# Prologue of a transformer block: packed constants, a short first norm, and batch 3's projections spread over the first scores

## The chip, the cores and the metric

The kernel runs as one program on one core of a Trainium2 chip. The core has TensorE (PE: matmuls; PEld: its weight loads), VectorE (DVE), ScalarE (ACT), GpSimd (POOL) and SyncE (SP), which here issues all DMAs. Each engine works through its own list of instructions in order and waits on semaphores. The metric is the time of one execution on the device, in microseconds (us), lower is better.

## What is computed

Attention with 16 heads of 8 over 16 batches of 256 tokens, width 128, then a mixture of experts, each with a norm ahead, a norm behind and a residual. Cut to what matters here:

```python
x = x + layernorm(attention(layernorm(x)))     # x: 16 x 256 x 128
x = x + layernorm(ffn(layernorm(x)))           # router, 32 experts, top 6, and a shared expert
# attention: q, k, v = xn @ w.T + b ; softmax(q k / sqrt(8)) v ; @ w_o.T + b_o
```

## The kernel before

**Tiles and batches.** `NB` = 16 batches of `T` = 256 tokens; a batch is `TH` = 2 tiles of 128 tokens. x stays in `xbig`. A batch has `NU` / `NB` = 2 units of scores, each of `UB` = 4 steps k with two heads packed into the array's halves, so that there are 32 units, u = 0 to 31.

**What a batch needs before its scores.** Normalise its two tiles (`norm_x`: `xn`), transpose them on PE (`transpose_x`, L1159, through `pX`), keep the result (`keep_xnT`, ACT), project q and k (L1164, L1167, both halves of the one bank `pX`). The float32 results are then cut into three bf16 parts: `part1` (ACT, L627 and L630), `rest` (DVE, L845, reads `pX` and writes `q_rest` and `k_rest`, of which there is one buffer each), `part2` (ACT for the first batches, POOL later), `part3` (L317, L318: on DVE for batches 0 and 1, on POOL from batch 2 on). SP writes the parts to DRAM (`write_parts`, L381, six DMAs) and reads them back in another layout as one unit of scores at a time (`load_unit`, L393, four DMAs, into a ring of `RING` = 6 slots).

**Scores are made twice.** `query_scores` (L1179, into three banks `pS1`) give the row maxima, which DVE takes (`row_max`, L865, two for each k). When a unit's eight maxima are there, POOL cuts them into parts (`split_max`, L499 to L502), PE transposes these (`transpose_max`, L1243, through `pX`), ACT copies them out (`keep_mT`), and SP puts them into the unit's slot (`load_max`, L401). Only then can `key_scores` (L1185) give the scores less their maxima, whose exponentials ACT takes (L655).

**The order, written out by hand.** PE projects batches 0 to 2, then computes query scores of units 0 to 2 (`LEAD` = 3). Among these lie `transpose_max(0)` behind k = 1 of unit 1, `project(3)` (all of batch 3's transposes and projections) behind k = 2 of unit 1, and `transpose_max(1)` behind k = 1 of unit 2. In the main loop, step j = 0 to 7 of batch b pairs key scores of unit 2b + j // 4 with query scores of unit 2b + 3 + j // 4; from j = 4 on there are also the outputs (L1235). So the loop's first step needs unit 3 in its slot, and j = 4 of batch 0 needs unit 4.

**SP's queue.** After the loads of x and of the constants: `write_parts(0)`, `load_unit(0)`, `load_unit(1)`, `write_parts(1)`, `load_unit(2)`, `load_max(0)`, `load_unit(3)`, `write_parts(2)`, `load_max(1)`, `load_unit(4)`, `load_unit(5)`, `write_parts(3)`, and so on (L404 to L436). `write_parts(b)` waits for `part3`, `load_unit(2b)` for the landing of b's parts, `load_max(u)` for `keep_mT(u)`.

**POOL's queue.** Memsets (the slots of the ring, `m_zero`, `power`, the pads, and the two large ones of `vv`, L489), the chain of the norm for batches 1 to 3 (`chain_x(0)`), `split_max(0)`, `part3(2)`, the chain for the batches from 4 on (`chain_x(1)`), `split_max(1)`, ...

**The first norm.** DVE takes the statistics of batch 0's tiles (L1041), then a chain of 20 small instructions (`norm_chain` with `fused=True`, L327 to L347), with an inverse root by three Newton steps; ACT normalises (L603).

## Time and profile before

| | |
|---|---|
| median of 3 runs | 531.38 us (530.69 to 531.44) |
| the profiled execution, its own time | 531.55 us |
| its span, first to last instruction | 529.5 us |
| mean granted TensorE clock | 0.994 |
| PE, busy share of the span | 91% |
| DVE, ACT, POOL | 76%, 67%, 32% |
| busy tenths of PE in the first four fortieths of the span | 2, 4, 5, 6 |
| the same, fifth fortieth to the end | nearly all 9 |

A fortieth is 13.2 us. The rows of the timeline give the start of an instruction, how long it took, the engine, the line, what it writes and reads; "x4" merges four in a row, and the square brackets tell how long the engine had been idle and what ended that. SPq is the queue on which SP issues DMAs: its rows are the issuing alone, the data move later.

### The profile page before, as it was taken

The page shows a single profiled execution, that of the slowest core. Times are in us where ns is not written, and L with a number is a line of the kernel's source. Part 1 is how long each engine was busy: PE and PEld are TensorE (multiplying, and loading weights), DVE is VectorE, ACT ScalarE, POOL GpSimd, SP SyncE. Part 2 cuts the span into 40 slices and gives each one's busy share as a digit, 9 for nine tenths or more (in the row PEclk, how much of TensorE's full clock was granted, in tenths as well). Part 3 has the DMA queues.
Part 4 walks back from the last instruction along what each step waited for, and adds up shares of the span by engine and source line. Part 5 has one row for each costly group of instructions (what it writes and reads, how often), then busy time and mean ns, then how long its engine had stood idle before and what let it go on. Part 6 is the DMA issues. An engine that isn't in the chain of part 4 may idle for free.

```text
span 529.5 us, 10851 instructions
## 1 busy us (share of the span) xinstructions
PE 479.3 (91%) x3376; PEld 268.1 (51%) x3376; DVE 400.7 (76%) x1074; ACT 354.9 (67%) x701; POOL 171.8 (32%) x501
## 2 busy tenths in 40 slices
PE   2456999999998999998799999999999999999994
PEld 1222445454444445444346666666656665666662
DVE  4678788899999989888926769596776859585453
ACT  2423788888889988887675566767667666755442
POOL 5045133333535535211002324425153533302021
PEclk9999999999999999999899999999999999999999
DMA  6334444444444344330042244535363544535431
GB/s 177 114 122 127 120 130 132 125 134 131 131 143 137 117 120 122 121 107 32 4 142 68 114 164 157 167 104 200 94 186 108 179 160 138 197 106 176 142 107 40
DMA packets 52744, 67.47 MB, mean 127 GB/s; under 512 B 4560, under 2 KB 36304, under 8 KB 52688
## 3 DMA queue, kind: packets, MB, share of 16 engines
q1 hardware_dynamic: 52688, 66.78, 40.5%
q8 instruction: 28, 0.46, 0.4%
q14 instruction: 28, 0.23, 0.2%
HBM read 51.17 MB, written 15.20 MB: 125 GB/s over the span
## 4 chain that ended last, share of the span: by engine, by line
PE 73%; DVE 9%; ACT 6%; issue 6%; POOL 5%; DMA 0%; POOLq 0%; DVEq 0%; ACTq 0%
PE pS L1316 12%; PE pY L1316 11%; PE pO L1235 8%; PE pS L1179 7%; PE pS L1300 6%; PE pS L1302 6%; PE pS L1301 6%; DVE mneg L865 4%; PE pS L1185 3%; ACT probs L655 3%; PE pX L1164 2%; PE pX L1167 2%; PE pX L1159 1%; PE pY L1262 1%; POOL xn L524 1%
## 5 line engine op out<-in xcount | busy, mean ns | idle before, releaser
L865 DVE TENSOR_REDUCE mneg<-pS 128x2 f32<-128x512 f32 x256 | 164.0, 685 | 23.4 <-PE pS L1179 22.7
L655 ACT ACTIVATE probs<-pS 128x512 f32<-128x512 f32 x256 | 144.2, 595 | 25.6 <-PE pS L1185 23.9
L730 ACT ACTIVATE h_ring<-r 128x512 f32<-128x512 f32 x144 | 90.4, 629 | 88.9 <-DVE r L1034 68.0
L1034 DVE SCALAR_TENSOR_TENSOR r<-pS,c_ring 128x512 f32<-128x512 f32 x128 | 87.6, 689 | 45.6 <-PE pS L1302 44.2
L1179 PE MATMUL pS<-kp,qp 48*128 48x256 bf16 x512 | 87.5, 291 | 18.8 <-DVE mneg L865 10.1
L1300 PE MATMUL pS<-qp,up_hi 128*128 128x512 f32 x144 | 103.5, 719 | 0.0
L1185 PE MATMUL pS<-qp,kp 51*128 51x256 bf16 x512 | 87.6, 282 | 0.9 <-ACT probs L655 0.7
L1235 PE MATMUL pO<-probs,vv 128*32 128x256 f32 x1024 | 74.1, 397 | 0.4 <-ACT oT_sb L606 0.4
L1316 PE MATMUL pS<-h_ring,down_sb 128*128 128x512 f32 x144 | 73.8, 594 | 0.0
L1316 PE MATMUL pY<-h_ring,down_sb 128*128 128x512 f32 x144 | 73.4, 595 | 0.0
L1179 PEld LDWEIGHTS pS<-kp,qp 48*128 48x128 bf16 x512 | 34.1, 96 | 69.0 <-DVE mneg L865 40.5
L1302 PE MATMUL pS<-qp,up_lo 128*128 128x512 f32 x144 | 57.0, 396 | 0.0
L1301 PE MATMUL pS<-kp,up_hi 128*128 128x512 f32 x144 | 56.7, 394 | 0.0
L1300 PEld LDWEIGHTS pS<-qp,up_hi 128*128 128x128 f32 x144 | 27.3, 189 | 27.3 <-issue 25.8
L1301 PEld LDWEIGHTS pS<-kp,up_hi 128*128 128x128 f32 x144 | 27.4, 190 | 26.4 <-issue 26.4
L499 POOL TENSOR_TENSOR m_parts<-mneg,m_zero 128x16 bf16<-128x16 f32 x32 | 7.0, 220 | 102.2 <-DVE mneg L865 102.2
L1235 PEld LDWEIGHTS pO<-probs,vv 128*32 128x32 f32 x1024 | 25.6, 110 | 27.1 <-issue 18.8
L1185 PEld LDWEIGHTS pS<-qp,kp 51*128 51x128 bf16 x512 | 33.0, 96 | 7.5 <-ACT probs L655 4.9
L545 POOL TENSOR_TENSOR xbig<-xbig,yn 128x512 f32<-128x512 f32 x8 | 10.5, 1311 | 67.0 <-ACT yn L603 67.0
L1316 PEld LDWEIGHTS pY<-h_ring,down_sb 128*128 128x128 f32 x144 | 27.0, 189 | 8.3 <-issue 1.4
L1316 PEld LDWEIGHTS pS<-h_ring,down_sb 128*128 128x128 f32 x144 | 27.1, 189 | 6.8 <-ACT h_ring L730 0.7
L1302 PEld LDWEIGHTS pS<-qp,up_lo 128*128 128x128 f32 x144 | 27.0, 188 | 6.0
(178 smaller groups left out, 679.0 us busy)
## 6 DMA issues: line engine op xcount, KB each, us to landing
c_ring<-c_scratch SPq DMA_DIRECT2D x64, 512.0 KB, 4.0
qp<-q_scratch SPq DMA_DIRECT2D x64, 96.0 KB
kp<-k_scratch SPq DMA_DIRECT2D x64, 96.0 KB
q_scratch<-q_parts SPq DMA_DIRECT2D x16, 192.0 KB, 2.3
k_scratch<-k_parts SPq DMA_DIRECT2D x16, 192.0 KB, 2.4
q_scratch<-q_parts SPq DMA_DIRECT2D x16, 128.0 KB, 2.2
k_scratch<-k_parts SPq DMA_DIRECT2D x16, 128.0 KB, 2.2
out_x<-ot SPq DMA_DIRECT2D x7, 256.0 KB, 4.4
```

The lines of the kernel that those rows point to most:

```text
L655: nc.scalar.activation(probs[j][:, hh], pS2[n % S2_RING][:, :, :], ACT.Exp, scale=SCALE).then_inc(exp_done, 1)
L730: nc.scalar.activation(h_sb[n % HRING], r_sb[n % URING][:, :], ACT.Square).then_inc(sq_done, 1)
L865: nc.vector.tensor_reduce(mneg[u % 2][:, :, hh, k], pS1[n % S1_RING][:, :].rearrange("p (a s) -> p a s", a=TH), AX.X, ALU.max, negate=True ...
L1034: nc.vector.scalar_tensor_tensor(out=r_sb[n % URING][:, :], in0=pU[n % URING], scalar=0.0, in1=c_ring[group % CRING][:, at], op0=ALU.max, ...
L1164: mm(pX[:, 0:T], wq_sb[:, :], xnT[b % 3][:, :], start=True, stop=True)
L1179: return mm(pS1[n % S1_RING][:, T * th:T * (th + 1)], qp[slot][rows, k, P * th:P * (th + 1)], kp[slot][rows, k, :], start=True, stop=True)
L1185: return mm(pS2[n % S2_RING][:, sh], kp[slot][rows, k, P * sh:P * (sh + 1)], qp[slot][rows, k, :], start=True, stop=True)
L1235: ins = mm(pO[VC * h:VC * (h + 1), g % 2], vv[b % 2][:, sh, 4 * g + h, :], probs[2 * g + h // 2][:, h % 2, sh, :], start=sh == 0, stop=sh ...
L1300: mm(bank, up_hi[:, block], x_hi[i % 2], start=True, stop=False)
L1301: mm(bank, up_hi[:, block], x_lo[i % 2], start=False, stop=False)
L1302: mm(bank, up_lo[:, block], x_hi[i % 2], start=False, stop=True).then_inc(up_done, 1)
L1316: mm(pF[i % 2], down_sb[:, block], h_sb[n % HRING], start=k == 0, stop=k == FBLK - 1).then_inc(down_done, 1)
```

## The change

- **Constants.** The identity, w_q, w_k and both of their biases come as one array in one DMA (`wqk`, 386 columns); w_v, w_o and their biases as one (`wvo`, 512 columns). Ahead of the large last load of x there were 12 DMAs and are now 5.
- **First norm.** DVE computes the variance in six small instructions, POOL takes the root of it with its power operation (`power` is now set first), DVE meanwhile subtracts the mean (one `scalar_tensor_tensor` over 128x256) and then scales the two tiles. ACT doesn't normalise batch 0 any more. POOL's other memsets, the two of `vv` among them, come behind the root.
- **part3** signals q and k apart, and SP starts to write q's parts without k's.
- **Batch 3.** `transpose_x(3)` moves behind k = 1 of unit 0, `project_q(3)` behind k = 2, `project_k(3)` behind k = 3; `rest(3)` on DVE from behind k = 3 of unit 1 to behind its k = 0.
- **Maxima.** `transpose_max(0)` moves from k = 1 of unit 1 to k = 3 (and now waits for `rest(3)`), `transpose_max(1)` from k = 1 of unit 2 to k = 2. On ACT `keep_mT(0)` comes behind batch 3's part1. SP's order stays.

```diff
@@ -301,7 +301,7 @@
         stored = [sem(f"stored{i}") for i in range(2)]
 
-        N_WQK, N_WA, N_WB = 5, 5, 1
+        N_WQK, N_WA, N_WB = 1, 2, 1
         N_PARTS = 16 * 6
@@ -314,7 +314,8 @@
 
             wait(part2_done, b + 1)
-            eng.tensor_tensor(q_parts[b % 2][:, 2], q_rest[:, :], q_parts[b % 2][:, 1], ALU.subtract)
+            eng.tensor_tensor(q_parts[b % 2][:, 2], q_rest[:, :], q_parts[b % 2][:, 1],
+                              ALU.subtract).then_inc(part3_done, 1)
             eng.tensor_tensor(k_parts[b % 2][:, 2], k_rest[:, :], k_parts[b % 2][:, 1],
@@ -351,23 +352,17 @@
             xd = x.rearrange("(n p) d -> p n d", p=P)
             sp.dma_start(xbig[:, 0:TH], xd[:, 0:TH]).then_inc(xq_loaded[0], 16)
-            sp.dma_start(idf[:, :], ident_f).then_inc(wqk_loaded, 16)
-            sp.dma_start(wq_sb[:, :], wq).then_inc(wqk_loaded, 16)
-            sp.dma_start(wk_sb[:, :], wk).then_inc(wqk_loaded, 16)
-            sp.dma_start(bqk_sb[:, 0:1], bq.unsqueeze(1)).then_inc(wqk_loaded, 16)
-            sp.dma_start(bqk_sb[:, 1:2], bk.unsqueeze(1)).then_inc(wqk_loaded, 16)
+            sp.dma_start(wqk_sb[:, :], wqk).then_inc(wqk_loaded, 16)
             sp.dma_start(xbig[:, TH:FIRST], xd[:, TH:FIRST]).then_inc(xq_loaded[1], 16)
-            sp.dma_start(wv_sb[:, :], wv).then_inc(wa_loaded, 16)
-            sp.dma_start(bv_sb[:, :], bv.unsqueeze(0).to_broadcast((P, D))).then_inc(wa_loaded, 16)
+            sp.dma_start(wvo_sb[:, :], wvo).then_inc(wa_loaded, 16)
             sp.dma_start(idb[:, :], ident_b).then_inc(wa_loaded, 16)
-            sp.dma_start(wo_sb[:, :], wo).then_inc(wa_loaded, 16)
-            sp.dma_start(bo_sb[:, :], bo.unsqueeze(0).to_broadcast((P, D))).then_inc(wa_loaded, 16)
             sp.dma_start(xbig[:, FIRST:NT], xd[:, FIRST:NT]).then_inc(xq_loaded[2], 16)
 
             def write_parts(b):
 
-                sp.wait_ge(part3_done, b + 1)
-                for parts, which, scratch in ((q_parts[b % 2], Q_PARTS, q_scratch), (k_parts[b % 2], K_PARTS, k_scratch)):
+                for i, (parts, which, scratch) in enumerate(((q_parts[b % 2], Q_PARTS, q_scratch),
+                                                             (k_parts[b % 2], K_PARTS, k_scratch))):
+                    sp.wait_ge(part3_done, 2 * b + i + 1)
                     s = 0
@@ -478,11 +473,14 @@
         def _(pool):
             nc.gpsimd.memset(tiny[:, 0:1], 0.0).then_inc(tiny_set, 1)
+            nc.gpsimd.memset(power[:, :], -0.5)
             for i in range(RING):
                 ins = nc.gpsimd.memset(kp[i][:, :, :].rearrange("p a b -> p (a b)").bitcast(F32), ONE_TWICE)
             ins.then_inc(ones_set, 1)
             nc.gpsimd.memset(m_zero[:, :, :, :], 0.0)
-            nc.gpsimd.memset(power[:, :], -0.5)
+            pool.wait_ge(ones_set, 1)
+            pool.wait_ge(var1_done, 1)
+            nc.gpsimd.tensor_tensor(rs1[:, 0:TH], nw_v[:, 0:TH], power[:, 0:TH], ALU.pow).then_inc(root1_done, 1)
             for tile, n in ((g_score, GROUPS), (g_best, TOPG), (masked, E), (e_best, TOPK)):
@@ -606,9 +604,8 @@
 
             def norm_x(b):
-                act.wait_ge(*((ln1_done, 1) if b == 0 else (ln1_rest_done, 1 if TH * b < FIRST else 2)))
-                if b >= 1:
-                    act.wait_ge(xnT_done, b)
+                act.wait_ge(ln1_rest_done, 1 if TH * b < FIRST else 2)
+                act.wait_ge(xnT_done, b)
                 for th in range(TH):
@@ -748,17 +745,16 @@
             nc.scalar.activation(tiny[:, 1:2], tiny[:, 0:1], ACT.Exp)
             act.wait_ge(wqk_loaded, 16 * N_WQK)
-            act.wait_ge(xq_loaded[0], 16)
             for b in range(AHEAD):
                 if b == 1:
                     act.wait_ge(xq_loaded[1], 16)
-                if b == AHEAD - 1:
-                    keep_mT(0)
-                norm_x(b)
+                if b >= 1:
+                    norm_x(b)
                 keep_xnT(b)
                 part1(b)
                 if b + 1 < AHEAD:
                     part2(b)
+            keep_mT(0)
             keep_mT(1)
@@ -840,7 +836,7 @@
                 dve.wait_ge(part1_done, b + 1)
                 if b >= 1:
-                    dve.wait_ge(part3_done, b)
+                    dve.wait_ge(part3_done, 2 * b)
                 for i, (left, parts) in enumerate(((q_rest, q_parts[b % 2]), (k_rest, k_parts[b % 2]))):
@@ -1040,9 +1036,20 @@
                 ins = nc.vector.bn_stats(stats[:, t, :], xbig[:, t])
             link(ins)
-            norm_chain(nc.vector, dve.wait_ge, link, stats[:, 0:TH],
-                       [w[:, 0:TH] for w in (nw_v, nw_t, nw_m, nw_d, nw_h)],
-                       rs1[:, 0:TH], nm1[:, 0:TH], fused=True).then_inc(ln1_done, 1)
+            even, odd = stats[:, 0:TH, 0:3], stats[:, 0:TH, 3:6]
+            d, m, v = (w[:, 0:TH] for w in (nw_d, nw_m, nw_v))
+            nc.vector.tensor_tensor(d, even[:, :, 1], odd[:, :, 1], ALU.subtract)
+            nc.vector.tensor_tensor(m, even[:, :, 1], odd[:, :, 1], ALU.add)
+            link(nc.vector.tensor_tensor(v, even[:, :, 2], odd[:, :, 2], ALU.add))
+            nc.vector.tensor_scalar(v, v, 1.0 / D, EPS, ALU.mult, ALU.add)
+            link(nc.vector.scalar_tensor_tensor(out=d, in0=d, scalar=0.25, in1=d, op0=ALU.mult, op1=ALU.mult))
+            nc.vector.tensor_tensor(v, v, d, ALU.add).then_inc(var1_done, 1)
+            link(nc.vector.scalar_tensor_tensor(out=xn[:, :, :], in0=m.unsqueeze(2).to_broadcast((P, TH, D)), scalar=-0.5,
+                                                in1=xbig[:, 0:TH], op0=ALU.mult, op1=ALU.add))
+            dve.wait_ge(root1_done, 1)
+            for th in range(TH):
+                ins = nc.vector.tensor_scalar(xn[:, th], xn[:, th], rs1[:, th:th + 1], None, ALU.mult)
+            ins.then_inc(xn_done, 1)
             dve.wait_ge(xq_loaded[1], 16)
@@ -1067,7 +1074,7 @@
                     for hh in range(2):
                         row_max(u, k, hh)
-                    if u == 1 and k == UB - 1:
+                    if u == 1 and k == 0:
                         rest(AHEAD - 1)
@@ -1340,14 +1347,18 @@
                 for k in range(UB):
                     scores_by_query(u, k)
-                    if u == 1 and k == 1:
+                    if u == 0 and k == 1:
                         pe.wait_ge(rest_done, AHEAD - 1)
+                        transpose_x(AHEAD - 1)
+                    if u == 0 and k == 2:
+                        project_q(AHEAD - 1)
+                    if u == 0 and k == 3:
+                        project_k(AHEAD - 1)
+                    if u == 1 and k == 3:
+                        pe.wait_ge(rest_done, AHEAD)
                         transpose_max(0)
-                    if u == 1 and k == 2:
+                    if u == 2 and k == 2:
                         pe.wait_ge(mT_kept, 1)
-                        project(AHEAD - 1)
-                    if u == 2 and k == 1:
-                        pe.wait_ge(rest_done, AHEAD)
                         transpose_max(1)
@@ -1476,24 +1487,19 @@
...
+        "wqk": np.concatenate([np.eye(P, dtype=np.float32), order(a["L0_attn_w_q"]).T, order(a["L0_attn_w_k"]).T,
+                               order(a["L0_attn_b_q"])[:, None], order(a["L0_attn_b_k"])[:, None]], axis=1),
+        "wvo": np.concatenate([a["L0_attn_w_v"].T, a["L0_attn_w_o"].T, np.broadcast_to(a["L0_attn_b_v"], (P, D)),
+                               np.broadcast_to(a["L0_attn_b_o"], (P, D))], axis=1),
```

## Rows read from the trace of the kernel before

**Rows 1.** The page: chain of work that ended last, shares by engine
```profile
PE 73%; DVE 9%; ACT 6%; issue 6%; POOL 5%; DMA 0%; POOLq 0%; DVEq 0%; ACTq 0%
```

**Rows 2.** Stretches: us; busy us (count) of PE, PEld, DVE, ACT, POOL; granted clock; DMA; GB/s
```profile
50.24:59.20 8.96, 8.96 (x70) 3.95 (x72) 5.52 (x10) 4.95 (x10) 2.21 (x7) 1.00 0.49 147
```

**Rows 3.** Timeline (start us, us, engine, line), first norm and first transpose
```profile
3.62 0.15 DVE L329 TENSOR_TENSOR nw_v<-stats 128x2 f32<-128x2 f32 x1
...
3.78 0.71 POOL L489 MEMSET vv<- 128x736 f32 x1
...
3.89 0.63 DVE L331 TENSOR_SCALAR nw_m<-nw_m 128x2 f32<-128x2 f32 x1
...
7.79 0.88 ACT L603 ACTIVATE xn<-xbig,nm,rs 128x128 f32<-128x128 f32 x2 [5.58 <-DVE nm L347]
...
8.82 0.66 PE L1159 MATMUL pX<-idf,xn 128*128 128x128 f32 x2 [8.82 <-ACT xn L603]
```

**Rows 4.** Timeline of the kernel's end: the last norm, with its root on POOL
```profile
524.22 0.16 DVE L1133 TENSOR_TENSOR work_v<-stats 128x4 f32<-128x4 f32 x1
...
524.91 1.02 POOL L597 TENSOR_TENSOR rs<-work_v,power 128x4 f32<-128x4 f32 x1 [3.52 <-DVE work_v L1136]
526.08 1.14 DVE L1146 SCALAR_TENSOR_TENSOR ot<-fn,rs,xbig 128x128 f32<-128x128 f32 x4 [0.64 <-POOL rs L597]
```

**Rows 5.** Groups by shape, POOL: xcount, busy us, mean ns, idle before
```profile
L339 POOL TENSOR_TENSOR rs<-nw_v,power 128x6 f32<-128x6 f32 x1 | 1.4, 1350 | 0.1
```

**Rows 6.** Groups by shape, DVE: a scale of 128x128 elements
```profile
L981 DVE TENSOR_SCALAR root_v<-score 128x128 f32<-128x128 f32 x1 | 0.3, 273 | 0.0
```

**Rows 7.** DMA issues: xcount, KB each, median us from issue to landing
```profile
xbig<-in_x SPq DMA_DIRECT2D x1, 384.0 KB, 3.3
...
xbig<-in_x SPq DMA_DIRECT2D x1, 128.0 KB, 2.2
```

**Rows 8.** Timeline, SP queue and the first scores
```profile
22.64 0.70 SPq L393 DMA_DIRECT2D kp<-k_scratch  x1
...
26.42 0.61 PE L1179 MATMUL pS<-kp,qp 48*128 48x256 bf16 x4 [0.98 <-DMA kp<-k_scratch]
```

**Rows 9.** Timeline, second unit of scores, on PE, ACT, POOL, DVE and SP
```profile
33.74 0.61 PE L1179 MATMUL pS<-kp,qp 48*128 48x256 bf16 x4 [0.85 <-DVE mneg L865]
...
34.28 0.39 PE L1243 MATMUL pX<-idb,m_parts 128*24 128x128 bf16 x2
...
34.51 0.67 POOL L318 TENSOR_TENSOR k_parts<-k_rest,k_parts 128x256 bf16<-128x256 f32 x1
...
34.71 0.37 ACT L606 ACTIVATE mT<-pX 24x256 bf16<-24x256 bf16 x1 [6.73 <-PE pX L1243]
...
35.42 1.61 SPq L401 DMA_DIRECT2D qp<-mT  x2
...
39.44 0.70 SPq L393 DMA_DIRECT2D kp<-k_scratch  x1
...
39.78 1.29 DVE L865 TENSOR_REDUCE mneg<-pS 128x2 f32<-128x512 f32 x2 [2.67 <-PE pS L1179]
...
40.98 0.48 DVE L845 SCALAR_TENSOR_TENSOR q_rest<-pX,bqk_sb,q_parts 128x256 f32<-128x256 f32 x1
...
41.77 1.28 DVE L865 TENSOR_REDUCE mneg<-pS 128x2 f32<-128x512 f32 x2
```

**Rows 10.** Timeline, SP queue, loads of the fifth unit
```profile
45.86 0.80 SPq L393 DMA_DIRECT2D qp<-q_scratch  x1
...
48.23 0.70 SPq L393 DMA_DIRECT2D kp<-k_scratch  x1
```

**Rows 11.** Timeline, main loop of batch 0: first key scores, first scores of j = 4
```profile
46.08 0.39 PE L1185 MATMUL pS<-qp,kp 51*128 51x256 bf16 x1
...
53.30 0.39 PE L1179 MATMUL pS<-kp,qp 48*128 48x256 bf16 x1
```

**Rows 12.** Timeline, PE, first scores after its step up in speed
```profile
59.84 0.28 PE L1179 MATMUL pS<-kp,qp 48*128 48x256 bf16 x1
```

More of the change, by code:

```diff
@@ L110, in __call__, with block_kernel @@
         self.eng.wait_ge(self.sem, self.base + self.n)
-def block_kernel(nc, x, wq, wk, wv, wo, bq, bk, bv, bo, route_in, up, shup, down, shdown,
-                 ident_f, ident_b, out):
+def block_kernel(nc, x, wqk, wvo, route_in, up, shup, down, shdown,
+                 ident_b, out):
     with ExitStack() as ctx:
@@ L133, in block_kernel @@
         ybig = sb("ybig", [P, NT, D])
-        wq_sb, wk_sb = sb("wq_sb", [P, D]), sb("wk_sb", [P, D])
-        wv_sb, wo_sb = sb("wv_sb", [P, D]), sb("wo_sb", [P, D])
-        bqk_sb = sb("bqk_sb", [P, 2])
-        bv_sb, bo_sb = sb("bv_sb", [P, D]), sb("bo_sb", [P, D])
+        wqk_sb, wvo_sb = sb("wqk_sb", [P, 3 * D + 2]), sb("wvo_sb", [P, 4 * D])
+        idf, wq_sb, wk_sb = (wqk_sb[:, D * i:D * (i + 1)] for i in range(3))
+        bqk_sb = wqk_sb[:, 3 * D:3 * D + 2]
+        wv_sb, wo_sb, bv_sb, bo_sb = (wvo_sb[:, D * i:D * (i + 1)] for i in range(4))
         route_sb = sb("route_sb", [P, E + C4 * E])
@@ L142, in block_kernel @@
         down_sb = sb("down_sb", [P, FBLK, D])
[L143 removed]
+        idb = sb("idb", [P, P], BF16)
         stats, stats2, stats3, stats4 = (sb(n, [P, c, 6]) for n, c in (
@@ L226, in block_kernel @@
         ones_set = sem("ones_set")
-        ln1_done = sem("ln1_done")
+        var1_done, root1_done = sem("var1_done"), sem("root1_done")
         ln1_stats = sem("ln1_stats")
@@ L1478 @@
         (0, 2, 3, 1) + tuple(range(4, 3 + w.ndim))).reshape(w.shape)
[L1479 to L1480 removed]
+    names = ["x", "wqk", "wvo", "route", "up", "shup", "down", "shdown",
+             "ident_b"]
     arrays = {
         "x": a["L0_attn_x"].reshape(NB * T, D),
[L1483 to L1490 removed]
+        "wqk": np.concatenate([np.eye(P, dtype=np.float32), order(a["L0_attn_w_q"]).T, order(a["L0_attn_w_k"]).T,
+                               order(a["L0_attn_b_q"])[:, None], order(a["L0_attn_b_k"])[:, None]], axis=1),
+        "wvo": np.concatenate([a["L0_attn_w_v"].T, a["L0_attn_w_o"].T, np.broadcast_to(a["L0_attn_b_v"], (P, D)),
+                               np.broadcast_to(a["L0_attn_b_o"], (P, D))], axis=1),
         "route": np.concatenate([a["L0_ffn_gate_w"].T] + [np.broadcast_to(a["L0_ffn_e_bias"], (P, E))] * C4, axis=1),
```

12 lines of the change are left out of this document (removed).

## The prediction

> **What bounds the kernel now.** I read the shares of the chain that ended last first: TensorE holds 73% of it, no other engine over 9% [rows 1]. The busy tenths then show that this isn't so at the start: PE is busy for 2 to 6 tenths in the first four slices, some 53 us, and for 9 from there on. The main loop of batch 0, from 46.08 on, is already full: from 50.24 to 59.20 PE is busy throughout [rows 2]. So a change of the prologue is worth just what it moves the first steps of the main loop by; behind them the order on PE is fixed and dense, and a shift is kept. The third view is the timeline of all engines from 0 to 62 us. Three things are to be seen. The chain of batch 0's norm runs on one engine at a time up to the first transpose at 8.82 [rows 3]. Scores come at the pace of PE and DVE by turns, and batch 3's projections cut a hole of 2.67 us into DVE's maxima [rows 9]. And SP's queue runs beside all that, with issues of 0.70 to 0.80 us each, nearly without a gap: behind the first maxima (35.42) come unit 3's loads (last one 39.44), six writes, and unit 4's loads (45.86 to 48.23) [rows 9, 10].
>
> **Step 1, the first norm.** DVE's third sum of the statistics starts at 3.62 [rows 3] and doesn't change. The kernel's end has the same new chain, sum to variance to POOL's root: from 524.22 to 524.91, 0.69 us [rows 4]. So the root starts at 3.62 + 0.69 = 4.31. It is a power of 2 columns; 4 columns took 1.02 [rows 4] and 6 took 1.35 [rows 5], 0.165 a column, so some 0.69: it ends at 5.00. DVE went on 0.15 behind such a root (1.02 + 0.15 = 526.08 - 524.91) [rows 4]: 5.15. Two scalings of 128x128, at 0.27 each alone [rows 6] and overlapped, end at 5.5. But POOL now starts its other memsets just there, and in the trace a DVE tensor_scalar of 2 columns beside a memset of vv (0.71 us) took 0.63 and ended with it [rows 3]. The first memset of vv would run from some 5.2 to 5.95; I let the scalings wait for it once: `xn` at 6.1, PE at 6.25 (PE started 0.15 behind ACT's norm, 7.79 + 0.88 to 8.82) [rows 3]. Before: 8.82. So S = 2.57 us are won; bounds 3.1 without a collision (5.5 + 0.15 to PE) and 1.8 if the second memset blocks too.
>
> **Step 2, packed constants.** Their 193 KB lie between x's loads of 128 KB (2.2 us to landing) and 384 KB (3.3) [rows 7]; issued at about 1.2 they are there by 4.5 at the latest, ahead of 6.25. Hidden, as the old ones were: nothing won but free time in SP's queue, in which nothing waits. The large load of x also starts earlier and is out of the way of the first parts. Splitting `part3`'s signal lets SP start about 0.3 earlier; SP isn't late at unit 0, so I price it at nothing beyond that, but `load_unit(2)` then ends near 32.5, some 2.9 earlier than 35.42.
>
> **Step 3, the first maxima.** Batches 0 to 2 follow the same chain of engines, so all shifts by S, and with it DVE's first maximum (it came behind `rest(2)`, no later than the scores of 26.42 allow) [rows 8]. From k = 0 of unit 0 (26.42) to k = 1 of unit 1 (33.74) five steps took 7.32: 1.464 each [rows 8, 9].
>
> **Step 4, batch 3 spread out.** PE is idle for 0.85 in each step [rows 9], and the transposes (0.66 in rows 3) fit into that; for each projection, some 1.0 by the hole itself (2.67 for transposes, a copy and two projections, partly in the usual gap), I take 0.07 of delay, 0.14 in all, an estimate: at worst 0.15 each. So the hole of 2.67, less the usual 0.17, goes: 2.5 us. That is what the edit is good for.
>
> **Step 5, the wait it adds.** `rest(3)` moves ahead to k = 0 of unit 1. It writes `q_rest`, which `part3(2)` on POOL still reads, and `part3(2)` stands behind `split_max(0)`, which needs all eight maxima of unit 0. Before, `part3(2)` ended at 34.51 + 0.67 = 35.18 and `rest(3)` began at 40.98 [rows 9]: no wait. Now it ends at 35.18 - 2.57 + 0.14 = 32.75. DVE would be ready at about 31.8: it stands for 1 us, with the maxima of unit 1 queued behind. `rest(3)` then starts at 32.79, the next maximum 0.79 later (40.98 to 41.77) [rows 9], at 33.58. Without both it would have started at 31.93: 1.65 lost.
>
> **Step 6, the maxima behind them.** `transpose_max(0)` was 0.54 behind the scores of k = 1 of unit 1, and SP came 1.14 later [rows 9]: at 35.42 SP had just finished `load_unit(2)`, ACT's copy being ready at 34.71 + 0.37 = 35.08. Now it stands two steps later. Those scores start at 33.74 + 2 x 1.464 - 2.57 + 0.14 + 1.65 = 35.89; the copy is ready 1.34 behind (35.08 - 33.74), SP issues at 37.25. That is 1.83 **later** than 35.42, although the prologue began earlier. Call this D. Everything behind it on SP is later by D: unit 3's loads, `write_parts(2)`, `load_max(1)`, unit 4's loads.
>
> **Step 7, where it lands.** A unit's scores can start 26.42 - 22.64 = 3.78 behind the issue of its last load, the one place where PE waited for it [rows 8]. Unit 3 was there at 39.44 + 3.78 = 43.2, long ahead of 46.08 [rows 9, 11]; now at 45.05. The scores themselves would let the main loop start at 35.89 + 5 x 1.464 = 43.2. So it starts at 45.05, 1.0 earlier than before. Unit 4 was there at 48.23 + 3.78 = 52.01 and needed at 53.30 [rows 10, 11]: a slack of 1.29. Now it is there at 53.84, while PE would come at 45.05 + 7.22 = 52.27. PE waits 1.6, and j = 4 starts at 53.84: 53.30 - 53.84 = -0.54. **The whole gain is given back in SP's queue, and half a microsecond more.** From there on units come in time: the next ones wait for the ring's slots.
>
> **Sum.** Span 529.5 + 0.54 = 530.04, with the 2.05 around it (531.55 - 529.5) 532.1. The profiled execution lies 0.17 over the median of 531.38, so against the median 531.9.
>
> **A rule against the change.** The trace shows the memset and the tensor_scalar ending together [rows 3]. The Trainium skill ("SBUF — State Buffer", section on SBUF's two sides) has VectorE and GpSimd share a port pair that one of them holds for a whole instruction, a VectorE operation with two SBUF inputs against a GpSimd one that reads too. By that rule the subtraction of the mean (two inputs, begun just ahead of the root) would hold the root up by some 0.3. That the memset blocked a tensor_scalar agrees with it; the other case no row of before shows.
>
> **The rivals.**
> A. *SP's queue takes the gain back* (forecast): +0.5; with S from 3.1 to 2.2 it is 0.0 to +0.9, so 531.4 to 532.4.
> B. *The main loop starts when the scores allow.* This needs loads that land sooner than 3.78 behind their issue. For: that figure is from one place. A plain 128 KB load landed in 2.2 [rows 7]; with 2.4 in place of 3.78 the result is 1.4 better than A, -0.9: 530.5. Against: the four loads of a unit are issued over 2.4 us and in the same order each time. With S at 3.1 as well 529.9. At most 2.9 (46.08 - 43.2) would be won, 528.5, were unit 4 no limit at all; its last issue would by itself be at 50.06, so this is shut out.
> C. *TensorE's clock, the other side.* The granted clock reads 1.00 [rows 2], but the scores of 256 columns took 0.39 at 53.30 and 0.28 at 59.84 [rows 11, 12], the first at the level of 1.2 GHz, the second at 2.4. The engine had been busy throughout since 50.24 before it rose near 59.2 [rows 2], 9.0 us. If A's idle 1.6 us ahead of j = 4 makes that stretch begin at 53.84, it rises near 62.8 in place of 59.2 while the work that was done cold till 59.2 takes as long: 3.1 us more at half speed, some 1.5 lost on top of A: 533.4. It decides once PE's idle time ahead of j = 4 is what restarts the stretch.
> D. *The port.* Both memsets of vv, or the root held up, make S 1.8: D is 2.6 and the result +1.3: 532.7.
> E. *The clock rises early.* PE is denser in the first unit than before (transposes and projections fill its gaps); if it went to 2.4 GHz there, each step of the scores gets about 0.3 shorter, and two or three steps lie on the path to `load_max(0)`: -0.6 to -1, so 530.9 to 531.3.
>
> **How the numbers follow.** A 0.50, B 0.13, C 0.17, D 0.10, E 0.10. The time is A's: 531.9. The range takes in B's 530.5 with some of S, and C: 530.2 to 533.4. A measurement of this kernel can tell about 0.2%, 1.06 us: faster is below 530.3, slower above 532.4. Faster: most of B and a bit of E, 0.14. Slower: C, most of D, and the edge of A: 0.30. The same: 0.56.
>
> **What would show it.** Step 1: the root on POOL starts at 4.3, `xn` ends between 5.5 and 6.9, the first transpose at 6.25. Step 4: no hole over 0.5 in DVE's maxima of unit 0. Step 5: DVE idle for about 1 us ahead of `rest(3)`, ended by POOL's L318. Step 6: the first L401 issue of SP at 37.3, behind an idle stretch of SP of over 4 us that ACT's copy ends. Step 7: PE waits for a load (unit 3) ahead of the first key scores at 45.05, and again for unit 4 ahead of j = 4 at 53.8. I am wrong if either wait isn't there, if SP issues unit 3's loads ahead of 37, or if the step up in PE's speed moves against j = 4 by more than a microsecond.

## The result, and the profile after

| | before | after |
|---|---|---|
| median | 531.0 us (530.68 to 531.44, 5 runs) | 536.33 us (534.74 to 540.23, 5 runs) |
| ratio after / before | | 1.0108, 95% interval 1.008 to 1.0137 |
| the profiled execution, its own time | 531.55 | 535.60 |
| its span | 529.5 | 533.3 |
| first transpose on PE | 8.82 | 7.04 |
| SP issues the first maxima (`load_max(0)`) | 35.42 | 38.38 |
| first key scores (the main loop starts) | 46.08 | 46.99 |
| j = 4 of batch 0, with the first outputs behind it | 53.30, 54.27 | 55.49, 56.46 |
| first scores at the fast level | 59.84 | 62.25 |
| DVE's `keep_y` of batch 0 | 75.36 | 77.76 |

The change made the kernel slower, by 1.1%, which is outside the range predicted (530.2 to 533.4). The sign at the place that I had worked out was right, +0.54 at j = 4; there it is +2.19, and 3.8 at the end of the span. The same kernel, run once more beside the last experiments (e9), was 0.6% slower.

The chain of work that ended last still names TensorE first, as in [rows 1]; the busy tenths of PE (40 slices of 13.3 us) still begin low:

```profile
PE 71%; DVE 9%; ACT 6%; issue 5%; POOL 5%; SPq 2%; DMA 2%; POOLq 0%; DVEq 0%; ACTq 0%
...
PE   2455899999999999998699999999999999999994
```

New in it are SPq with 2% and DMA with 2% (was 0%): SP's queue and the loads behind it now stand on the chain. The tenths show an 8 and a 6 near the middle, where PE is short of work (an 8 and a 7 at the same spot of before); that spot comes back below.

The timeline at the first norm, to be read against [rows 3] and [rows 4] (start, us, engine, line):

```profile
4.16 0.42 DVE L1047 SCALAR_TENSOR_TENSOR xn<-nw_m,xbig 128x256 f32<-128x256 f32 x1
...
4.39 0.74 POOL L483 TENSOR_TENSOR rs<-nw_v,power 128x2 f32<-128x2 f32 x1 [0.70 <-DVE nw_v L1046]
...
5.24 1.65 DVE L1051 TENSOR_SCALAR xn<-xn,rs 128x128 f32<-128x128 f32 x2 [0.67 <-POOL rs L483]
...
5.24 0.70 POOL L487 MEMSET vv<- 128x736 f32 x1
...
5.95 0.70 POOL L487 MEMSET vv<- 128x736 f32 x1
...
7.04 0.66 PE L1166 MATMUL pX<-wqk_sb,xn 128*128 128x128 f32 x2 [7.04 <-DVE xn L1051]
```

The two scalings start together with the first memset of `vv` and end 0.24 behind the second: 1.65 us for two instructions that took 0.27 each alone [rows 6]. The timeline of the second unit of scores and of SP's queue, to be read against [rows 9], [rows 10] and [rows 11]:

```profile
33.17 0.67 POOL L319 TENSOR_TENSOR k_parts<-k_rest,k_parts 128x256 bf16<-128x256 f32 x1
...
33.94 0.48 DVE L841 SCALAR_TENSOR_TENSOR q_rest<-pX,wqk_sb,q_parts 128x256 f32<-128x256 f32 x1 [0.85 <-POOL k_parts L319]
...
37.56 0.39 PE L1250 MATMUL pX<-idb,m_parts 128*24 128x128 bf16 x2
...
38.38 1.61 SPq L396 DMA_DIRECT2D qp<-mT  x2
...
42.40 0.70 SPq L388 DMA_DIRECT2D kp<-k_scratch  x1
...
43.14 2.59 SPq L376 DMA_DIRECT2D q_scratch<-q_parts  x3
...
46.99 0.39 PE L1186 MATMUL pS<-kp,qp 48*128 48x256 bf16 x1 [3.46 <-DMA kp<-k_scratch]
...
51.60 0.70 SPq L388 DMA_DIRECT2D kp<-k_scratch  x1
...
55.49 0.39 PE L1186 MATMUL pS<-kp,qp 48*128 48x256 bf16 x1 [1.48 <-DMA kp<-k_scratch]
```

Here one sees the whole turn. The transposes of the first maxima are at 37.56, where they were at 34.28; SP issues behind ACT's copy at 38.38, having stood idle since 32.73; unit 3's last load follows at 42.40; and PE, ready for the main loop, stands for 3.46 us for it. Unit 4's last load is issued at 51.60 (was 48.23), and PE stands once more, for 1.48 us.

### The profile page after: what moved, and what is told of

Its sections match the earlier page's. It is cut to its first block, busy times and chain, and to the rows that moved or that the text cites. A ratio compares the mean times of both kernels' runs of the same rounds, so it can differ in the third digit from the quotient of the medians.

```text
span 533.3 us, 10834 instructions
## 1 busy us (share of the span) xinstructions
PE 479.3 (90%) x3376; PEld 268.2 (50%) x3376; DVE 399.9 (75%) x1063; ACT 353.8 (66%) x699; POOL 172.5 (32%) x502
## 4 chain that ended last, share of the span: by engine, by line
PE 71%; DVE 9%; ACT 6%; issue 5%; POOL 5%; SPq 2%; DMA 2%; POOLq 0%; DVEq 0%; ACTq 0%
PE pS L1323 12%; PE pY L1323 11%; PE pO L1242 9%; PE pS L1307 6%; PE pS L1309 6%; PE pS L1308 6%; PE pS L1186 6%; PE pS L1192 3%; DVE mneg L861 3%; ACT probs L652 2%; PE pX L1171 2%; PE pY L1269 1%; PE pX L1174 1%; PE pX L1166 1%; POOL xn L522 1%
```

## The experiments

**Theory**, after the result: the prologue's end is set by SP's queue, whose order puts unit 3's loads and batch 2's writes behind `load_max(0)`; the spread work makes those maxima late. **Rivals**: the time goes into TensorE's clock (its step up after the prologue), or into something in the body of the kernel that only goes with the changed code. Four milestones are used for every kernel: the first transpose, the issue of `load_max(0)`, the first key scores and the first outputs (all in us of its profiled execution). The medians are compared with runs of before taken beside them: 531.53 (26 runs) for e1 to e4, 531.24 (35) for e5 to e8, 530.98 (23) for e9 to e12. The ratio in the last column isn't the quotient of the two medians; it can differ from that by up to 0.002 (e5, 1.0026, where the medians give 1.0047), which is about as much as the intervals reach to one side (0.9 to 1.5 us).

| kernel | transpose | `load_max(0)` | key scores | outputs | median (runs) | ratio to before, 95% |
|---|---|---|---|---|---|---|
| before | 8.82 | 35.42 | 46.08 | 54.27 | | |
| after | 7.04 | 38.38 | 46.99 | 56.46 | 536.33 (5) | 1.0108 [1.008, 1.0137] |
| e1 SP's order | 7.03 | 39.27 | 42.96 | 51.15 | 529.87 (12) | 0.9965 [0.9939, 0.999] |
| e2 norm only | 6.94 | 33.27 | 44.23 | 52.42 | 529.59 (12) | 0.9958 [0.9942, 0.9975] |
| e3 spread only | 9.09 | 40.92 | 48.99 | 58.49 | 536.35 (6) | 1.0081 [1.0056, 1.0106] |
| e4 three repairs | 5.90 | 38.43 | 41.71 | 49.59 | 527.47 (9) | 0.9924 [0.9897, 0.9951] |
| e5 memsets later | 5.85 | 37.19 | 45.53 | 54.83 | 533.72 (12) | 1.0026 [1.0002, 1.005] |
| e6 part3 first | 6.90 | 37.30 | 45.43 | 55.23 | 533.15 (12) | 1.0019 [0.9996, 1.0043] |
| e7 delay 2 | 11.07 | 37.10 | 48.07 | 56.26 | 533.14 (12) | 1.0018 [0.9995, 1.0042] |
| e8 delay 1 | 10.02 | 36.31 | 47.27 | 55.46 | 532.32 (12) | 1.0007 [0.9983, 1.0032] |
| e9 after again | 6.92 | 38.00 | 46.16 | 55.93 | 534.56 (6) | 1.006 [1.0036, 1.0084] |
| e10 norm, memsets later | 5.76 | 32.10 | 43.06 | 51.25 | 529.04 (12) | 0.996 [0.994, 0.9979] |
| e11 hold SP long | 8.81 | 40.98 | 49.00 | 58.30 | 536.57 (5) | 1.0097 [1.0071, 1.0123] |
| e12 hold SP short | – | 36.97 | 45.90 | 54.11 | 532.56 (12) | 1.0033 [1.0009, 1.0056] |

### e1: only SP's order

The changed kernel, with one line of SP's queue moved.

```diff
             load_unit(2)
-            load_max(0)
             load_unit(3)
             write_parts(2)
+            load_max(0)
             load_max(1)
```

> The changed kernel with one edit in SP's order: unit 3's loads and write_parts(2) ahead of load_max(0), instead of behind it. Theory (SP's queue stands behind the first maxima): SP issues unit 3's loads from about 32.8 us on without a wait, the main loop starts at 44.4, when the scores allow it (46.99 in the changed kernel), PE waits for no load ahead of j = 4, which starts at 51.6 (55.49 there, 53.30 before); 1.7 us faster than before, some 529.3. Rival (the clock or the DMAs' own speed takes the time, not the order in which SP waits): 534 or more, as the changed kernel.

The maxima were issued even later than in the changed kernel (39.27), and yet the main loop began 4.03 earlier (42.96 against 46.99) and the first outputs came 5.31 earlier. Both were some 1.4 us earlier than I had expected: the main loop at 42.96 and not 44.4, j = 4 at 50.18 and not 51.6. SP's timeline:

```profile
39.27 4.47 SPq L396 DMA_DIRECT2D qp<-mT  x4
```

Both units' maxima now go out together, behind unit 3's loads and batch 2's writes. The waits that one instruction leaves on another (us in all, count, longest; 30 to 60 us), first of the changed kernel, then of e1:

```profile
PE pS L1186 <- DMA kp<-k_scratch: 4.9, 2, 3.5
```

```profile
PEld pS L1186 <- DMA kp<-k_scratch: 0.3, 1, 0.3
```

The two waits of 3.46 and 1.48 shrink to one of 0.3. The cause of the loss at the first outputs is the order of SP's queue, and with it in order the whole change is a gain over before, 0.35% by the ratio. That is no more than the norm alone gives (e2, below, 0.42%): of the 3.12 us by which the first outputs came earlier than before, the median shows 1.66.

### e2 and e3: each half of the change alone

e2 is the changed kernel with the prologue's order on PE, DVE and ACT as before; e3 is the kernel before with the changed order.

```diff
-                    if u == 0 and k == 1:
-                        pe.wait_ge(rest_done, AHEAD - 1)
-                        transpose_x(AHEAD - 1)
...
+                    if u == 1 and k == 1:
+                        pe.wait_ge(rest_done, AHEAD - 1)
+                        transpose_max(0)
+                    if u == 1 and k == 2:
+                        pe.wait_ge(mT_kept, 1)
+                        project(AHEAD - 1)
...
```

> The kernel before with the packed constants and the short first norm alone; batch 3 and the maxima stand where they stood. Theory: SP's queue has no wait behind it that is longer than before, so the 1.78 us by which the first transpose is earlier reach j = 4 of batch 0 (51.5): 529.2 us. Rival (the gain of a shorter start is lost in any case, in DMA or in the clock): within 0.5 us of before.

> The kernel before with batch 3's spreading and the transposed maxima behind it alone; old constants, old first norm. Theory: without the 1.78 us of the norm, load_max(0) is issued near 40.2 (35.42 before), unit 4 comes some 4 us late, j = 4 starts near 57.3: 535 us. Rival (the spreading wins its hole of 2.5 us, and the loss comes from the norm's side): 528.5 to 530.

Against before the first outputs moved by 52.42 - 54.27 = -1.85 with the norm alone, and by 58.49 - 54.27 = +4.22 with the spread alone; together +2.37, and both at once gave +2.19. The halves add up, as far as one trace each can say: the changed kernel's own first outputs lay between 55.93 and 56.46 in four traces. The norm's share is its S whole (8.82 - 6.94 = 1.88), since every step behind it moved along. e3's timeline shows the spread's own damage, without the help of an early norm:

```profile
36.48 0.48 DVE L844 SCALAR_TENSOR_TENSOR q_rest<-pX,bqk_sb,q_parts 128x256 f32<-128x256 f32 x1 [0.86 <-POOL k_parts L318]
...
40.92 1.59 SPq L401 DMA_DIRECT2D qp<-mT  x2
```

DVE stands 0.86 for POOL, as in the changed kernel, and SP issues the maxima at 40.92 in place of 35.42: 5.50 later, of which the first outputs feel 4.22; 1.29 is the slack of unit 4 that step 7 had counted, 5.50 - 1.29 = 4.21. (Two small terms cancel in this: unit 4's last load was issued 12.72 behind the maxima and not 12.81, and landed in 3.89 and not 3.78.)

### e4: SP's order, the memsets and part3 together

```diff
+            pool.wait_ge(xn_done, 1)
             for tile, n in ((g_score, GROUPS), (g_best, TOPG), (masked, E), (e_best, TOPK)):
...
-                split_max(u)
                 if u == 0:
                     part3(nc.gpsimd, pool.wait_ge, 2)
+                split_max(u)
+                if u == 0:
                     chain_x(1, FIRST, NT)
```

and e1's move on SP.

> The changed kernel with three edits: SP's order as in the first run; POOL's memsets behind the first norm's xn, so that they don't meet its scalings; part3(2) on POOL ahead of split_max(0), so that rest(3) needn't wait. Theory: xn ends at 5.5 instead of 6.9 (1.3 won), rest(3) doesn't wait for POOL (0.85 won): main loop at about 42.3, j = 4 at 49.5, 3.8 us faster than before, 527.2. Rival (something further on in SP's or POOL's queue ends last): between 527.5 and 529.5, with a wait of PE for a load or for POOL's split_max(1) ahead of the main loop.

527.47 against 531.53: ratio 0.9924, faster than both kernels and the best of all that ran. The first outputs are at 49.59, 4.68 ahead of before and 6.87 ahead of the changed kernel. The first key scores now wait for the maxima instead of for the loads:

```profile
38.43 3.49 SPq L396 DMA_DIRECT2D qp<-mT  x4
...
41.70 0.37 PE L1188 MATMUL pS<-kp,qp 48*128 48x256 bf16 x1 [0.51 <-DMA qp<-mT]
```

PE's wait there is 0.51, in place of the changed kernel's 3.46.

### e5 and e6: the memsets and part3, one at a time

e5 is the changed kernel with POOL's wait for `xn_done` alone; e6 is it with `part3(2)` ahead of `split_max(0)` alone (the two hunks of e4).

> The changed kernel, with POOL's small memsets and those of vv made to wait for the first norm's xn, so that they can't meet its scalings. Theory (the memsets hold VectorE's scalings): the two scalings take 0.4 us in place of 1.65, the first transpose starts at 5.75 (7.04 in the changed kernel), load_max(0) is issued at 37.1 (38.38), j = 4 of batch 0 starts 1.3 earlier, at 54.2: 535.0 of 536.3. Rival (the scalings are slow by themselves, by their pointer operand): 7.04 and 536.3, unchanged.

> The changed kernel with one edit in POOL's order: part3(2) ahead of split_max(0). Theory (rest(3) waits for part3(2)): DVE's wait of 0.85 us ahead of rest(3) is gone, load_max(0) is issued at 37.5 (38.38), j = 4 starts at 54.6 (55.49): 535.4. Rival (DVE's wait is covered by something else, PE's pace or part1(3) on ACT): load_max(0) stays at 38.4 and the time at 536.3.

In e5 the scalings have DVE's side to themselves:

```profile
5.22 0.48 DVE L1052 TENSOR_SCALAR xn<-xn,rs 128x128 f32<-128x128 f32 x2 [0.67 <-POOL rs L483]
...
5.85 0.66 PE L1167 MATMUL pX<-wqk_sb,xn 128*128 128x128 f32 x2 [5.85 <-DVE xn L1052]
```

0.48 instead of 1.65, with the same start and the same operands; only the memsets were taken from beside them. The 1.17 came through to PE (7.04 to 5.85, 1.19) and to SP (38.38 to 37.19, 1.19). In e6 `rest(3)` begins at 32.87 with no wait, and SP issues 1.08 earlier:

```profile
32.87 0.47 DVE L842 SCALAR_TENSOR_TENSOR q_rest<-pX,wqk_sb,q_parts 128x256 f32<-128x256 f32 x1
...
37.30 1.59 SPq L396 DMA_DIRECT2D qp<-mT  x2
```

So the wait that step 5 named cost 1.08 at SP and 56.46 - 55.23 = 1.23 at the outputs; the memsets cost 1.19 and 1.63. The prices at the outputs hold to about half a microsecond, the spread of the changed kernel's own traces there (55.93 to 56.46). With either repair alone the ratio to before is 1.002 to 1.003 (the medians are 1.9 and 2.5 us above), and with neither is it below 1: with SP's order as it is both only make the same load less late. Both medians were better than expected, 533.15 and 533.72 and not 535.4 and 535.0.

### e7 and e8: before, with the prologue delayed

17 and 11 further statistics instructions on DVE ahead of the first norm, in the kernel before; they write to a tile that is overwritten later.

```diff
             dve.wait_ge(xq_loaded[0], 16)
+            for n in range(17):
+                nc.vector.bn_stats(fn[:, 0, 6 * n:6 * n + 6], xbig[:, 0])
```

> The kernel before with 17 extra statistics of 0.2 us each on DVE ahead of the first norm; they delay it by 3.4, of which 1.0 comes back since POOL's memsets of vv are then over when the norm's scalings come: batch 0 to the end 2.4 later, and nothing else changed. If the changed kernel's last 1.4 us (3.8 in its span, 2.4 up to the keep_y of batch 0 at 75 us) come from where in time the clock of TensorE falls, this kernel loses some 1.5 as well: 3.9 over before, 534.9 to 535.4. If they come from something the change does to the middle of the kernel, this one loses 2.4 only: 533.4 to 533.9.

> The same with 11 extra statistics: 1.2 later at the end of the prologue. If only the shift counts: 532.2 to 532.7. If the place in time of the clock's fall counts, up to 1.5 more, or up to 1 less.

These ask whether a shift of the main loop has a price beyond itself. The first outputs came 1.99 and 1.19 later, the medians 1.90 and 1.08 (533.14 and 532.32 against 531.24). A pure shift of 2 us costs about 2 us; the agreement to 0.1 is closer than the runs can tell, since the intervals of the two ratios reach some 1.3 us to either side. The execution of e7 that was traced was the slowest of its twelve (535.37); what it lost is below. e7's first outputs (56.26) are where the changed kernel's are (56.46), but the changed kernel's medians stand 1.7 to 3.4 us further above their before (e9: 3.58 - 1.90; first result: 5.33 - 1.90). This spoke against "the shift brings the rest along", and sent me back to the body of the kernel.

### e9: the changed kernel once more

> The changed kernel once more, beside the others. Its trace was 2.4 us behind that of before at 75 us and 3.8 at the end, and its five times spread from 534.7 to 540.2. If 2.4 is what the change costs and the rest comes and goes with the clock: a median of 533.4 to 534.2. If the whole 3.8 or more belongs to the change: 535 to 536.5.

534.56 in the median of 6, 3.58 above before beside it; ratio 1.006. That lies between the two forecasts and decides for neither. Outputs at 55.93, so +1.66 there. All 11 executions of the changed kernel timed so far were at 533.8 or above; of the 35 of before beside e5 to e8, 9 were over 533.

### e10: the norm with its collision taken away

e2 with e5's wait on POOL.

> The packed constants and the short first norm alone, as in the second experiment, with POOL's memsets behind the first norm: first transpose at 5.85 (7.04 there). Theory: no wait of SP takes this back; another 1.2 us: 528.3 to 528.6. Rival (the gain is capped by SP's queue, which is now late by itself): 529.6, as the second experiment.

529.04. The first transpose moved from 6.94 to 5.76 and the outputs from 52.42 to 51.25, 1.17 more; but the ratio stays at 0.996, where e2 had 0.9958. The gain is in the prologue and not in the median, within an interval of some 2 us. Its trace lost nothing behind batch 0 (-0.12 by the measure explained below); of the 1.1 that are missing 0.25 lies outside the span (below), and the rest in executions that no trace shows.

### e11 and e12: before, with only SP held

The kernel before, in which SP waits for a later maximum of DVE ahead of `load_max(0)`; 15 (e11) or 14 (e12).

```diff
             load_unit(2)
+            sp.wait_ge(max_done, 15)
             load_max(0)
```

> The kernel before, with SP made to wait ahead of load_max(0) until 15 of the first 16 maxima are there (some 40.5 us in place of 35.4); nothing else. Theory: D = 5.1, less unit 4's slack of 1.3: PE waits for unit 3 until about 48.3 and for unit 4 until 57.1, 3.8 us slower, 535.0. Rival (a wait of SP in the prologue is hidden by the units in the ring): 531.2.

> The same with 14 of 16 maxima (some 37.1 us): D = 1.7. Theory: unit 3 in time, unit 4 just late, PE waits 0.4 us ahead of j = 4: 531.6. Rival as above: 531.2 and no wait of PE for a DMA.

e11 gives the kernel before the changed kernel's two waits, with one wait of SP added:

```profile
40.98 1.59 SPq L401 DMA_DIRECT2D qp<-mT  x2
...
49.00 0.39 PE L1180 MATMUL pS<-kp,qp 48*128 48x256 bf16 x1 [2.39 <-DMA kp<-k_scratch]
...
57.33 0.39 PE L1180 MATMUL pS<-kp,qp 48*128 48x256 bf16 x1 [1.30 <-DMA kp<-k_scratch]
```

SP 5.56 later, PE waits at the same two places for the same loads, and j = 4 is at 57.33, 4.03 later; the slack of 1.29 and D = 5.56 give 57.57, an error of 0.24. The median rose by 5.59. In e12, with D = 1.55, PE hardly waits (0.3 for a load, 0.4 had been expected) and the outputs are at 54.11, 0.16 earlier than before: there is nothing of the hold to be seen in the prologue. But its median is 1.58 over before's.

### e13 to e16: before and after, in turn, on one chip

> The kernel before once more, for its trace alone. If the clock's fall in batches 13 to 15 is by chance free of cost in the one trace of before that was read, other executions of it lose 1 to 3 us between 75 us and the end (against that trace); if it is free because of where the kernel stands in time, they lose 0 to 0.3.

> The changed kernel once more, for its trace alone. Its two traces lost 1.4 and 3.6 us between 75 us and the end. If that is tied to the kernel: over 1 again. If it is chance: anything from 0 to 4, as in the kernel before.

> As the kernel before's other trace: 0 to 0.3 between 75 us and the end if it is tied to the kernel, 0 to 4 if it is chance.

> As the changed kernel's other trace: over 1 if it is tied to the kernel, 0 to 4 if it is chance. In both, first outputs of batch 0 at 55.9 to 56.5, which is the part that SP's queue makes.

Unchanged kernels, each with a trace of its own (time around the trace, outputs, `keep_y` of batch 0, span):

| | time | outputs | fast scores behind outputs | `keep_y` | span |
|---|---|---|---|---|---|
| e13, before | 530.57 | 54.24 | 3.46 | 74.43 | 528.6 |
| e15, before | 530.31 | 54.23 | 3.19 | 74.14 | 528.3 |
| e14, after | 532.98 | 56.09 | 3.84 | 76.65 | 530.8 |
| e16, after | 532.92 | 56.22 | 3.65 | 76.58 | 530.7 |

The difference is 2.22 and 2.44 at `keep_y` and 2.2 and 2.4 at the end. In these four executions the whole loss of the span is the prologue's, and none comes behind it. The times differ by 0.2 more (2.41 and 2.61), and this part is found in every execution: those of the kernels with the packed constants and the short norm (after, e1, e2, e4, e5, e6, e9, e10, e14, e16) took 2.17 to 2.30 us outside their span, those of the others 1.93 to 2.07. Which edit makes it, no run shows.

### Where the remainder goes

`keep_y` of batch 0 is a good place to part the kernel in two. I take span less `keep_y`, against the same of before (529.5 - 75.36 = 454.14): what an execution lost behind batch 0. After: 533.3 - 77.76 - 454.14 = 1.40. e9: 3.70; e14 and e16: 0.01 and -0.02; e13 and e15: 0.03 and 0.02; e7: 2.93; e8: 0.13; e12: 4.60. So it is a matter of the single execution, from nothing to 4.6 us, in either kernel. The `keep_y` of all 16 batches show where it is lost: most of it in two places. (Ahead of batch 0's `keep_y` there is a third: the step up in speed came 5.57 behind the first outputs in the first trace of before and 3.19 in e15, and with the same outputs, 54.27 and 54.23, `keep_y` was at 75.36 and 74.14, 1.2 apart, as are the spans.)

**The first place: maxima that SP loads late.** Between `keep_y` of batches 11 and 12 (233 to 249 in before) seven traces lost 0.8 to 3.2 us (e2 0.78, e6 0.79, e4 1.06, e11 1.07, e12 2.22, e7 2.48, e9 3.22). In these seven, and in no other, PE waits 1.56 to 2.48 us there for a load of maxima; in the other eleven this wait is 0.43 at most. In e9, the changed kernel's second trace (timeline):

```profile
225.54 0.36 ACT L604 ACTIVATE mT<-pX 24x256 bf16<-24x256 bf16 x1
...
232.98 1.57 SPq L396 DMA_DIRECT2D qp<-mT  x2
...
235.97 0.27 PE L1186 MATMUL pS<-kp,qp 48*128 48x256 bf16 x1 [2.48 <-DMA qp<-mT]
```

ACT's copy of the maxima is ready at 225.90, and SP issues their load at 232.98, 7.08 behind, since it first works through four loads of a unit and six writes of a batch. In e4 and e7 it is 6.32 and 5.96, in e14, where PE doesn't wait, 3.39. It is the prologue's pattern once more, a small load behind larger ones in SP's queue, and it is in kernels made from either one. Why SP is further behind in one execution than in another, no run shows. The stretches (us; busy us and count of PE, PEld, DVE, ACT, POOL; granted clock; DMA; GB/s) show PE idle there, and behind it the granted clock falls:

```profile
234.00:236.00 2.00, 0.03 (x2) 0.06 (x4) 0.28 (x1) 0.34 (x1) 0.88 (x4) 1.00 0.04 13
...
236.00:238.00 2.00, 2.00 (x24) 0.88 (x24) 1.29 (x2) 1.46 (x3) 0.00 (x0) 0.58 0.26 76
```

It did so behind this wait in e7, e9 and e12, which lost 2.2 to 3.2 us here; where it didn't, the wait cost 0.8 to 1.1.

**The second place: where the clock falls.** Between `keep_y` of batches 13 and 14 (266 to 276 in before) six traces lost 0.7 to 2.3 us. The stretches ahead of it, first in before, which lost nothing, then in the changed kernel:

```profile
254.00:256.00 2.00, 0.47 (x4) 0.42 (x4) 1.93 (x8) 0.67 (x2) 0.00 (x0) 1.00 0.02 6
...
258.00:260.00 2.00, 2.00 (x20) 0.59 (x16) 1.80 (x7) 1.08 (x2) 0.00 (x0) 0.50 0.03 8
```

```profile
256.00:258.00 2.00, 0.33 (x3) 0.33 (x4) 1.93 (x9) 0.82 (x2) 0.00 (x0) 1.00 0.02 6
...
262.00:264.00 2.00, 0.33 (x8) 0.00 (x0) 1.83 (x8) 0.78 (x2) 0.00 (x0) 1.00 0.00 0
...
268.00:270.00 2.00, 2.00 (x20) 0.53 (x16) 1.22 (x3) 0.20 (x2) 0.00 (x0) 0.50 0.00 0
```

In the middle of the changed kernel PE has two holes of some 1.7 us in which DVE is nearly full (1.93 and 1.83 of 2.00), and behind the second PE's granted clock falls to 0.50 for some 3.4 us. In before it fell at 257 to 260, behind the first hole (254 to 256), in a stretch in which DVE (1.80) holds PE up anyway: `keep_y` was 75.36 against 77.76, +2.40, and the shift was 2.15 at 249 and 2.13 at 265. In the changed kernel it fell behind the second hole, at 266 to 269, where DVE has room again (1.22): at 276 the shift is 3.65. The same fall costs nothing at one spot and 1.5 at the other.

All 18 traces have such a fall between 252 and 273, and they sort by it. Twelve have one of some 3.4 us that begins between 252 and 262, and lost nothing here. The six that lost have one that begins at 265 to 266 (after and e5, 1.5 each), one of twice the length, 6.8 us (e2 0.78, e3 0.73, e1 2.25), or both (e12 2.26). That is still a correlation, since no run here changed the falls alone.

Against the shift of the outputs, the medians of e2, e7 and e8 carry no extra (-0.1 us each), those of e3 and e4 0.6, those of e1, e5, e6, e10, e11 and e12 0.9 to 1.9, and those of the changed kernel 3.1 and 1.9; 0.25 of it is outside the span in the kernels named above. The extra does not follow the shift: e12 has none and pays 1.7. Whether the changed kernel meets the two places more often is not shown. Of 84 executions of before beside the experiments, 21 had a lower mean granted clock than the others (0.983 to 0.990, or 0.948 where the record of the prologue reads 0.50 as well); 19 of these were at 533.1 to 537.1, and of the other 63 all but one below 532.7. Of the changed kernel's 11 executions five had such a lower mean (0.990, 0.948, 0.942), at 535.7 to 540.2, and six had not, at 533.8 to 535.6. Five of 11 against 21 of 84 is too few to tell the two kernels apart.

## Why the prediction was right and wrong

**Step 1, the norm, half right.** The root was predicted at 4.31 and 0.69 long, and was at 4.39 and 0.74. The first scaling was predicted at 5.15 and began at 5.24. The length of the scalings was wrong: I let them wait for one memset, and they met both, so S was 8.82 - 7.04 = 1.78, not 2.57. Rival D had this value (S = 1.8); I gave it a chance of 0.10. [Rows 3] had shown one small instruction ending with one memset, and there were two instructions and two memsets to come; together they took as long as both memsets. The Trainium skill ("SBUF — State Buffer", section on SBUF's two sides) has VectorE and GpSimd share a port pair that one holds for a whole instruction; 1.65 against 0.48 in e5 agrees with it. By the same rule the two-input subtraction at 4.16 should have held the root. The trace shows no such hold: the root started at 4.39 while the subtraction ran until 4.58, and took 0.74, as in every kernel with this norm, where [rows 4] and [rows 5] had let expect 0.69. A hold until 4.58 would have made it some 0.88, an estimate; spans on GpSimd are rough, so that a hold of 0.05 isn't excluded.

**Step 2, the constants, right inside the span.** Nothing waited for them, and SP was done earlier (its first write at 13.42 instead of 15.48), which nothing used. But the sum kept the 2.05 us outside the span as they were, and they became 2.2 to 2.3 in every kernel with this half of the change: a term of 0.25 that was put at nothing.

**Step 4, the hole, right in kind and too cheap.** The hole is gone. But the three steps with work put into them took 1.61, 1.69 and 1.70 us (scores at 26.16, 27.77, 29.46 and 31.16) where 1.464 was the pace: 0.61 of delay, not 0.14. That PE was idle for 0.85 a step did not make these 0.85 free: I had taken the transposes as wholly hidden and the projections as all but hidden, at 0.07 each.

**Step 5, the wait, right.** Predicted 1 us, ended by POOL's `part3`; it was 0.85, and e6, which takes away what it waits for, priced it at 1.08 on SP.

**Step 6, the step that failed in size.** D was to be 1.83 and was 38.38 - 35.42 = 2.96. Of the 1.13 more, 0.79 is S and some 0.5 is step 4, less a little at step 5. The mechanism was as said: SP idle for 5.65 (predicted over 4), ended by ACT's copy.

**Step 7, again right in mechanism.** PE waits for unit 3 and again for unit 4, the two places named. Three sizes were off. Unit 3's loads landed 42.40 to 46.99, 4.59 behind the last issue, not 3.78, and unit 4's 55.49 - 51.60 = 3.89. The issue of q's three writes took 2.59 instead of 1.53. Of this 1.06 an idle stretch of SP ahead of the second maxima took up some 0.6 (43.29 to 43.96 in before), so that unit 4's last load was late by 3.37, 0.41 more than D. This part belongs to the one execution: in e9 the writes took 1.53 and in e14 2.43, and in both the last load came 12.8 behind `load_max(0)`, as in before. Why the issue stretches, no run shows; loads of a unit were under way in before as well. With these the same sum is 3.37 (issue) + 0.11 (landing, 3.89 - 3.78) - 1.29 (slack) = 2.19, which is what j = 4 shows (55.49 - 53.30). My bound of 3.78 from the one place where PE had waited was the smallest of these three landings, and I used it as if it had no spread; over the experiments they lie between 3.70 (unit 4 in e11) and 4.59.

**Behind j = 4, an assumption that didn't hold.** This is the second step that failed. I wrote that behind the first steps of the main loop a shift is kept, the order on PE being fixed and dense. In four traces of the changed kernel 1.66 to 2.19 at the outputs became 1.2 to 4.4 at the span's end. In e7 and e8 the medians kept it to 0.1. So it holds for many executions, and single ones add a loss of 0 to 4.6 us on top: a wait of PE for late maxima near 235 (2.48 in e9) and a fall of the clock near 266 (1.5 in the first trace of after). The order is dense, but PE still depends on SP's queue in it. The range was built from rows of a single execution and had no term for it: of the 5.33 by which the medians differ, 2.19 are at j = 4, 0.25 outside the span, and the other 2.9 are of this kind.

**The rivals.** B (the loads land sooner) did not come, they landed later. C, the clock's step up restarted by the idle ahead of j = 4, was refuted: from the first outputs to the first fast scores it took 5.57, 3.46 and 3.19 us in three traces of before, without that idle time, and 5.79, 3.42, 3.84 and 3.65 in four of after, with it. One spread, in both kernels. E (the clock rises early) did not come: four scores of the first unit took 0.61, and those of 46.99 and 55.49 0.39, as before. D was the rival that occurred, by its memsets; its 532.7 was too low as well, for it kept the other terms. Two slips in the sums changed nothing: A's upper end is 531.38 + 0.9 = 532.3, not 532.4, and a root held up by 0.3 would by itself have left S at 2.3, not 1.8.

**What stays.** The change costs 1.7 to 2.2 us at the first outputs, and that is shown, by e1 (taken away by SP's order alone), e11 (made by SP alone) and e3. Another 0.25 lies outside the span, in every execution. The remaining 1.7 to 2.9 us of the medians' difference (3.58 and 5.33) come from single executions: in the traces they go with PE's wait for late maxima near 235 and with where and how long the clock falls. In the two traces taken in turn with before nothing of it is seen, and whether the changed kernel meets it more often is open.

## What to carry to other kernels

When work is moved ahead in a hand-written order, look at what was moved behind it, and then at every in-order queue that waits for that: here a load that needed nothing of the late maxima stood behind them on SP, and to move one line of the queue turned a loss of 0.6 to 1.1% into a gain of 0.35%. The same queue made PE wait for late maxima in the middle of the kernel too, so look at it there before the clock is blamed. A wait's slack covers a delay only up to its size; price each transfer behind it by a range of landings (3.7 to 4.6 us here) rather than by the one that PE happened to wait for. And put a memset on GpSimd behind the short VectorE chain it runs beside, not next to it.
